# Starting the expert loops of a fused transformer kernel once their first groups of tokens are routed

## The reference, cut to what matters

```
# experts (stages 0 and 2)
logits = x @ router_w.T                         # [T, 8]
m1 = max(logits); gates1 = softmax(where((m1-logits)/max(|logits|,m1) > 0.02, -inf, logits))
mult1 = gates1[argmax]                          # the same once more without the winner: mult2
dense_w[tok, ind1] += mult1; dense_w[tok, ind2] += mult2
for e in range(8):
    h = silu(x @ w_gate[e].T) * (x @ w_up[e].T)             # 128 -> 256
    out += dense_w[:, e:e+1] * (h @ w_down[e].T)            # 256 -> 128
x = x + 0.5 * out                                # the kernel puts the 0.5 into the gates
# attention (stage 1), 16 heads of 8
attn = softmax(q k^T * 8**-0.5); out = (attn v) @ w_proj.T + b_proj
```

## Time and profile before

| | us |
|---|---|
| median of 3 executions | 2050.31 |
| the profiled execution | 2053.51 |
| its span, first to last instruction | 2051.7 |
| stage 0, front and routing | 0 to 65 |
| stage 0, expert loops | 65 to 361 |
| attention, preparation | 361 to 421 |
| attention, turns 0 to 15 | 421 to about 1097 |
| attention, turn 16 | about 1097 to 1145 |
| attention's end, front and routing of stage 2 | 1145 to 1207 |
| stage 2, expert loops | 1207 to 1507 |
| stages 3 to 5 | 1507 to 2052 |

### The profile page before, as it was taken

How to read it: one execution, slowest core, us unless ns; L and a number is a source line. 1 busy time by engine, 2 the same in 40 slices (tenths; PEclk the granted TensorE clock), 3 DMA queues, 4 the chain that set the end, 5 groups by cost and what they waited for, 6 DMA issues and landing times.

```text
span 2051.7 us, 31351 instructions
## 1 busy us (share of the span) xinstructions
PE 1710.9 (83%) x10673; PEld 980.1 (48%) x10673; DVE 1498.2 (73%) x2427; ACT 936.7 (46%) x1787; POOL 407.4 (20%) x716
## 2 busy tenths in 40 slices
PE   4799999549998999899898569999967669885675
PEld 3688888301111111111112358888845545553454
DVE  4655555689999999999992366555668848886884
ACT  2222222506887888788787322222234412111452
POOL 5311010310000100000000310100035642333442
PEclk9999999858999999999999769999987869997787
DMA  3000000210100011001100100000000000000000
GB/s 114 1 1 0 0 0 1 97 57 18 41 23 22 22 34 30 22 22 29 27 16 8 51 0 1 0 0 0 0 1 0 0 1 1 1 1 1 1 21 21
DMA packets 25450, 35.17 MB, mean 17 GB/s; under 512 B 6016, under 2 KB 20160, under 8 KB 24832
## 3 DMA queue, kind: packets, MB, share of 16 engines
q1 hardware_dynamic: 25344, 33.79, 5.6%
HBM read 20.80 MB, written 8.39 MB: 14 GB/s over the span
## 4 chain that ended last, share of the span: by engine, by line
PE 65%; DVE 17%; issue 5%; POOL 5%; ACT 5%; DMA 1%; POOLq 1%; DVEq 0%; SPq 0%; ACTq 0%
PE PS L744 12%; PE PS L312 11%; PE PS L732 9%; PE PS L301 6%; PE PS L302 6%; PE PS L303 6%; PE PS L721 5%; DVE neg_half L844 4%; DVE shared L1528 3%; PE PS L1281 3%; ACT probs L812 3%; DVE qk_all L1063 2%; PE PS L1393 1%; PE PS L1295 1%; DVE qk_all L1066 1%
## 5 line engine op out<-in xcount | busy, mean ns | idle before, releaser
L844 DVE TENSOR_REDUCE neg_half<-PS 128x2 f32<-128x1024 f32 x512 | 601.0, 1220 | 48.0 <-PE PS L721 33.1
L812 ACT ACTIVATE probs<-PS 128x512 f32<-128x512 f32 x1024 | 529.2, 604 | 184.8 <-PE PS L732 184.4
L363 ACT ACTIVATE shared<-PS 128x512 f32<-128x512 f32 x256 | 153.1, 598 | 425.9 <-PE PS L303 409.9
L477 DVE TENSOR_TENSOR shared<-shared,PS 128x512 f32<-128x512 f32 x256 | 175.8, 687 | 173.2 <-ACT shared L363 172.8
L732 PE MATMUL PS<-qk_all 51*128 51x512 bf16 x1024 | 279.7, 391 | 16.9 <-ACT probs L812 12.2
L744 PE MATMUL PS<-probs,Vg 128*32 128x512 f32 x2048 | 277.8, 615 | 0.1
L721 PE MATMUL PS<-qk_all 48*128 48x512 bf16 x1024 | 203.3, 408 | 60.4 <-DVE neg_half L844 39.4
L312 PEld LDWEIGHTS PS<-wd,shared 128*128 128x128 f32 x2048 | 247.9, 192 | 11.5
L312 PE MATMUL PS<-wd,shared 128*128 128x128 f32 x2048 | 248.6, 275 | 0.0
L732 PEld LDWEIGHTS PS<-qk_all 51*128 51x128 bf16 x1024 | 72.3, 94 | 343.5 <-ACT probs L812 326.1
L485 DVE SCALAR_TENSOR_TENSOR x<-PS,gates,x 128x128 f32 (+1 forms) x512 | 144.2, 344 | 72.7 <-PE PS L312 72.7
(11 more groups left out here) (194 smaller groups left out, 2321.8 us busy)
## 6 DMA issues: line engine op xcount, KB each, us to landing
split<-shared SPq DMA_DIRECT2D x16, 384.0 KB, 3.3
qk_all<-split SPq DMA_DIRECT2D x64, 96.0 KB
qk_all<-split SPq DMA_DIRECT2D x64, 64.0 KB
qk_all<-split SPq DMA_DIRECT2D x64, 32.0 KB
shared<-OTs SPq DMA_DIRECT2D x60, 32.0 KB
SC<-OTs SPq DMA_DIRECT2D x60, 32.0 KB
probs<-in_ret_const SPq DMA_DIRECT2D x1, 1538.5 KB, 6.8
qk_all<-negT SPq DMA_DIRECT2D x96, 4.0 KB, 1.8
```

The costliest lines, as they stand in the source:

```text
L363: act.activation(sg[:, f, :], bank(f), ACT.Silu).then_inc(s["silu"], 1)
L477: dve.tensor_tensor(h[:, FCH * (e % 2) + f, :], sg[:, f, :], bank(2 + f), ALU.mult).then_inc(s["h"], 1)
L812: act.activation(probs[:, n % 2, STRIPS * strip + pair, :], bank(RING_AT + use % RING), ACT.Exp, scale=ATT_SCALE).then_inc(s["exped"], 1)
L844: dve.tensor_reduce(neg_half[m % 2][:, i % 2, :, at], bank(use_bank(i, m), 2).rearrange("p (s w) -> p s w", s=STRIPS), AX.X, ALU.max, nega ...
```

## The change

- **The front.** Only the first 2 groups (stage 0) or 4 groups (stage 2), `HEAD`, are normalised, transposed, scored and routed ahead of the loops. The others pass through `first_group`, the loop over the 8 experts of group 0, at places given by `FRONTS`; one PSUM bank each for transposes (6) and logits (7). In stage 0 that is two groups in each of the experts 0, 1, 2; in stage 2 groups 4, 5, 6, 7 in experts 1, 2, 3, 5. The rest of the routing is a generator stepped on DVE in experts 4 to 7 (3, 3, 3, 4 steps) in stage 0 and 6, 7 (9, 4) in stage 2. Logits are taken from `xT`; the second copy `xTf` is gone.
- **Stage 2's head** lies in attention's turn 16, between its steps. The projection, addition and statistics of groups 6 and 7, and the last half's reciprocal, move into experts 0, 1 and 2 of `first_group`. POOL's `ln_finish` is written out between its attention work.
- **Routing.** The two rounds share one exponential over both; operations that do not depend on each other are not chained; two parts (head, rest).
- **Weights of stage 0.** hi and lo are made in 4 chunks of 512 columns, POOL's chunks alternating with `ln_finish` of two groups; x arrives in two transfers, the second behind the weights.
- **Reciprocals** of sequences 0 to 2. SP moves one row of denominators per head to DRAM, gathers 16x1024 into 128x128, DVE takes that reciprocal in turns 6, 10, 14 (step 1), SP writes it to DRAM and spreads it onto 128x1024; POOL multiplies in turns 7, 11, 15.
- FP4 weight steps go beside groups 6 and 7 of stage 2 in place of 0 and 7.

```diff
+        HEAD = {0: 2, 2: 4}
+        FRONTS = {0: {0: (2, 3), 1: (4, 5), 2: (6, 7)}, 2: {1: (4,), 2: (5,), 3: (6,), 5: (7,)}}
@@ moe_pe @@
+            def first_group():
+                left = None
+                for e in range(EXPERTS):
+                    if e + 1 < EXPERTS:
+                        if n == 0 and (e + 1) % 2 == 0:
+                            pe.wait_ge(ld["wlo"], e + 3)
+                        gate_up(0, e + 1, FCH * e + 1)
+                    else:
+                        pe.wait_ge(s["lo"], 2)
+                        gate_up(1, 0, FCH * e + 1)
+                    if left is not None:
+                        moe_logits(pe, n, left, 7)
+                        left = None
+                    fronts = FRONTS[n].get(e, ())
+                    if fronts:
+                        if n == 2:
+                            pe.wait_ge(att["added"], GROUPS - 1 if e < 3 else GROUPS)
+                        moe_transposes(pe, n, fronts[0], 6)
+                    down(0, e)
+                    if fronts:
+                        moe_logits(pe, n, fronts[0], 7)
+                    if len(fronts) > 1:
+                        moe_transposes(pe, n, fronts[1], 6)
+                        left = fronts[1]
+                    if n == 2 and e == 0:
+                        att_project(pe, GROUPS - 2, 6)
+                    if n == 2 and e == 2:
+                        pe.wait_ge(s["xT"], FRONTS[2][2][0] + 1)
+                        att_project(pe, GROUPS - 1, 6)
@@ moe_dve @@
+            def first_group():
+                rest = route(dve, chain, n, 1, s["gates"])
+                for e in range(EXPERTS):
+                    wait(dve, s["y"], e)
+                    hidden(e + 1, (e + 1) % EXPERTS)
+                    add(0, e)
+                    if n == 0 and e == 0:
+                        for g in range(4, GROUPS):
+                            ln_stats(dve, g)
+                    if n == 2 and e in (0, 2):
+                        g = GROUPS - 2 + e // 2
+                        att_add(dve, g, 6)
+                        dve.wait_ge(att["added"], g + 1)
+                        ln_stats(dve, g)
+                    if n == 2 and e == 1:
+                        att_reciprocals(dve, BATCH - 1, GW, SEQ)
+                    for g in FRONTS[n].get(e, ()):
+                        moe_scores(dve, n, g, 7)
+                    if e + 1 > n // 2:
+                        for g in FRONTS[n].get(e + 1, ()):
+                            moe_tokens(dve, n, g)
+                    for _ in range({0: (0, 0, 0, 0, 3, 3, 3, 4), 2: (0, 0, 0, 0, 0, 0, 9, 4)}[n][e]):
+                        next(rest)
...
+            head = route(dve, chain, n, 0, s["x_acc"])
+            for _ in range(9):
+                next(head)
             hidden(0, 0)
+            for _ in head:
+                pass
+            for g in FRONTS[n][n // 2]:
+                moe_tokens(dve, n, g)
+            first_group()
@@ moe_pool, stage 0 @@
+                for c in range(W_CHUNKS):
+                    weights_low(c)
+                    if c < W_CHUNKS - 1:
+                        ln_finish(pool, 0, 2 * c + 2)
+                        ln_finish(pool, 0, 2 * c + 3)
+                moe_low(pool, 0, 1)
@@ att_sp @@
+            def gather_sums(b):
+                sp.wait_ge(s["moved"], MOVED * HG * (b + 1))
+                wait(sp, s["spread"], 16 * b)
+                sp.dma_start(compact_sums[:, :], sums[b, :, :].rearrange("h (k w) -> (h k) w", k=HD)).then_inc(s["sums"], 16)
+            def spread_inverse(b):
+                sp.wait_ge(s["rec"], b + 1)
+                sp.dma_start(inverse[b, :, :].rearrange("h (k w) -> (h k) w", k=HD), compact_sums[:, :]).then_inc(s["inverse"], 16)
+                sp.wait_ge(s["inverse"], 16 * (b + 1))
+                wait(sp, s["on"], b)
+                sp.dma_start(SC[:, 0, :], inverse[b, :, :].unsqueeze(1).to_broadcast([HEADS, HD, SEQ])).then_inc(s["spread"], 16)
...
+                if i > HG and i % HG == 2:
+                    spread_inverse(i // HG - 1)
                 if 1 < i <= AG:
+                    r = i - 2
+                    if r < AG - HG:
+                        compact(r)
+                    else:
+                        compact_wide(r, 0, SEQ, s["moved"])
@@ att_pe, steps n of turn 16, g = n // 2 @@
+                        if n % 2 == 0 and 4 <= g < 4 + HEAD[2]:
+                            moe_logits(pe, 2, g - 4, LOGITS[2])
+                        if n % 2 == 0 and 3 <= g < 3 + HEAD[2]:
+                            moe_transposes(pe, 2, g - 3, TURNED[2])
@@ att_pool, after its loop @@
+            for g in range(HEAD[2]):
+                ln_finish(pool, 2, g)
+            moe_low(pool, 2, 0)
+            ln_finish(pool, 2, HEAD[2])
+            ln_finish(pool, 2, HEAD[2] + 1)
+            normalised(BATCH - 1, BATCH, 0, GW)
+            moe_low(pool, 2, 1)
+            ln_finish(pool, 2, GROUPS - 2)
+            normalised(BATCH - 1, BATCH + 1, GW, SEQ)
+            ln_finish(pool, 2, GROUPS - 1)
```

More of the change, by code:

```diff
@@ new lines, in moe_copy, with moe_logits @@
+        def moe_copy(act, n, g, b):
+            act.wait_ge(moe[n]["xT_ps"], g + 1)
+            act.activation(xT[:, g * GW:(g + 1) * GW], bank(b), ACT.Copy).then_inc(moe[n]["xT"], 1)
+        def moe_logits(pe, n, g, b):
+            s = moe[n]
+            pe.wait_ge(s["xT"], g + 1)
+            wait(pe, s["logits"], g)
+            for j in range(GT):
+                t = g * GT + j
+                last = pe.matmul(bank(b)[:, j * EXPERTS:(j + 1) * EXPERTS], xT[:, t * P:(t + 1) * P], wr[:, :],
+                                 start=True, stop=True)
+            last.then_inc(s["logit_ps"], 1)
@@ L271, in moe_pe @@
         def moe_pe(pe, n):
             s = moe[n]
-            def transposes(g, u):
-                pe.wait_ge(s["xn"], g + 1)
-                wait(pe, s["xT"], g - 1)
-                for j in range(GT):
-                    last = pe.transpose(bank(6 + u)[:, j * P:(j + 1) * P], xn[:, u, j * P:(j + 1) * P], ident[:, :])
-                last.then_inc(s["xT_ps"], 1)
-            def logits(g, u):
-                if more(g):
-                    transposes(g + 1, 1 - u)
-                pe.wait_ge(s["xTf"], g + 1)
-                wait(pe, s["logits"], g - 1)
-                for j in range(GT):
-                    last = pe.matmul(bank(4 + u)[:, j * EXPERTS:(j + 1) * EXPERTS], xTf[:, u, j * P:(j + 1) * P],
-                                     wr[:, :], start=True, stop=True)
-                last.then_inc(s["logit_ps"], 1)
@@ L290, in moe_pe @@
-            transposes(0, 0)
-            rolled(pe, logits)
             def gate_up(g, e, ready):
@@ L505, in moe_dve @@
+            for _ in head:
+                pass
+            dve.wait_ge(s["x_acc"], 1)
+            for g in FRONTS[n][n // 2]:
+                moe_tokens(dve, n, g)
+            first_group()
+            dve.wait_ge(s["gates"], 1)
+            before = GROUPS - 2 if n == 2 else GROUPS - 1
+            with dve.Fori(1, before) as g:
                 group(g, False)
-            group(GROUPS - 1, True)
+            for g in range(before, GROUPS):
+                group(g, g == GROUPS - 1)
             dve.wait_ge(s["x_acc"], E_LAST + 1)
@@ L746, in values @@
                 last.then_inc(s["pv"], 1)
-            def project(g):
-                pe.wait_ge(s["on"], max(g // 2, g - BATCH + 1) + 1)
-                pe.wait_ge(s["read"], len(NUMBER))
-                wait(pe, s["added"], g - JH + 1)
-                for j in range(GT):
-                    t = g * GT + j
-                    last = pe.matmul(bank(g % JH)[:, j * P:(j + 1) * P], OC[:, t * P:(t + 1) * P], wproj[:, :],
-                                     start=True, stop=True)
-                last.then_inc(s["proj"], 1)
             def turn(i, first, second, third):
@@ L1653, in _ @@
             ln_stats(dve, 0)
-            for name, first, last in (("x_half", 1, GROUPS // 2), ("x_rest", GROUPS // 2, GROUPS)):
-                dve.wait_ge(ld[name], 16)
-                with dve.Fori(first, last) as g:
-                    ln_stats(dve, g)
-            dve.wait_ge(ld["small"], 32)
+            ln_stats(dve, 1)
             moe_dve(dve, chain, 0)
```

355 lines of the change are left out of this document (221 added, 134 removed).

## The result

The changed kernel took 1977.49 us (median of four executions, 1976.24 to 1979.08), the kernel before 2050.56: a ratio of 0.9638, 95% interval 0.9626 to 0.9651. The forecast was 1976 (1959 to 2000). Run again beside later experiments, the changed kernel took 1981.2 (five executions, 1974.96 to 1987.97; ratio 0.9658, 0.9634 to 0.9681); of those 3.7 us more, 3.2 are in the kernel before too, which took 2053.7 beside it. What is its own is the spread: 13 us, against 3 us for the kernel before. That turned out to be the most interesting thing in this case.

What follows compares the result with a forecast made beforehand. Expert loops are PE-bound and unchanged; serial time in two routing fronts and three reciprocals goes: 20.9 + (22.8 - 3) + (38.5 - 2.5) = 76.7, less 2 unseen, off 2050.3 gives 1976 us, range 1959 to 2000.

Steps and rivals of the forecast that it cites:

- Reciprocals: 20.9 said: Attention, sequences 0 to 2: removing three wide reciprocals saves 23.9 us, three small ones cost 1.0 each; gain 20.9.
- 0.95 x 7.95 / 6.54: Attention: most that one added 128x128 reciprocal loses, scaled from the wide one's cost; 1.2 us, taken as 1.0.
- rival 2: Attention: compact reciprocals' transfers land late, 4 us at each of three sequences; 1988 us, or 1997 at worst; chance 0.07.
- Stage 0: 19.8 said: Stage 0: fourth add gains 25.2 us, 2.4 lost to the rest of routing, 3 to clock restarts.
- the fourth add of group 0 comes at 62.8: Stage 0: after POOL's chain come normalisation, h of expert 3, gate-up, logits, down; add at 62.8, today 87.99.
- Two engines, one port: Stage 0: POOL's operations hold DVE's routing operations for up to 1.26 us each; 0 to 3 us, taken as 1.5.
- the last part: List of signs in the trace; for stage 0, wrong if PE's idleness before the fourth add ends on anything but POOL's rstd.
- The clock's 3: Stage 0: one and a half TensorE clock restarts of about 2 us each, charged as 3 us.
- Turn 16 and stage 2: 36.0 said: Attention's end to group 1's second add: at 1219.9, today 1258.36; gain 38.5 us less 2.5 for clock restarts.
- Rival 1: First groups' expert loops crawl at half clock with queue waits: 36 us more, 2012; half of it, 1994, likelier; chance 0.16.
- Rival 3: Stage 0: late x transfer and POOL's serial chain keep the first group as late as today; 1996 us; chance 0.12.
- rival 4: Expert loops: TensorE stays at its low clock level after the first group, 56 experts x 4.1 us; 2206 us; chance 0.02.

Runs made afterwards that it cites:

- the two reciprocal kernels: Changed kernel with 128x1024 reciprocals put back for sequences 0 to 2, 2004.0 us; changed kernel with three more 128x128 reciprocals ahead of each compact one, 1993.2 us.
- logits apart: Changed kernel with the logits of turn 16's first three groups issued one step later, between the halves of the transposed scores; 1973.9 us, ratio 0.9634.
- fill: Changed kernel with three more 512-column matmuls ahead of the logits of each of the four groups in turn 16; 1986.0 us, ratio 0.9680.

## Why the prediction was right, and where it was not

The time was right, 1976 for 1977.5 (and 1981.2 later), and the mechanism was right: serial time in two fronts and three reciprocals, taken away while the loops stayed PE-bound. Its terms were less exact than its sum, and that the sum came out within 2 us was in part luck: stage 0 gave 5.5 us less than was said; the reciprocals and stage 2 gave 3.6 more, and the 2 us kept for things unseen were not needed.

- **Reciprocals: 20.9 said, 23.1 measured.** Removing them was worth what the half sets said, as the experiment that puts them back shows. The small one was charged 1.0 us each time and cost 0.17: DVE had that much slack. The sum was linear ("0.95 x 7.95 / 6.54"); measured were 0.17 for the first and 3.6 to 4.9 for the next three. (The row of 0.61 us that the prediction reads as one matmul covers two.) The transfers' room of 7.4 us was enough (rival 2 did not occur): the spread was issued at 671.19 and the evacuation at 680.03 was on time.
- **Stage 0: 19.8 said, 14.3 measured in the first profile, 16.5 to 17.0 in the repeated and the two reciprocal kernels (second add of group 1 at 98.7 to 99.1).** The step that failed is "the fourth add of group 0 comes at 62.8". The schedule followed POOL's queue to the rstd of group 7 and stopped there, "the end is 55". Behind it POOL goes on: a weight chunk, a lower half, two memsets of 5.26 us, and DVE's normalisation of exactly the groups that were just made ready lies beside them. The prediction had this effect in hand ("Two engines, one port") and charged 1.5 us for small operations in the routing; it didn't look for the large ones. Before, the memsets lay beside the loops and cost nothing. POOL's rstd was there at 51.5 and PE was idle until 60.71, for DVE's `xn` that the memset held; the last part had named any other end of that wait than rstd as a sign of being wrong.
- **It came out near because other terms were too dear.** Independent routing operations start 0.14 to 0.16 us apart (21.26, 21.40 and then 21.62, 21.76, 21.92, 22.05), only chained ones 0.26, so the head's routing ended at 25.8 and not at 27.5. POOL's chain from group 4 to 7 took 15.4 and not 16.5. The rest of the routing cost 0.95 and not 2.4 (28.58 us from the fourth add to the second of group 1, 27.63 before; by the prediction's own 0.40 us an operation the last expert's nine are 1.15 over and not 0.9). The clock's 3 were partly not needed: behind the first h TensorE worked at 1.2 GHz only for some 7 us of group 0, 47.0 to 50.4 and 60.7 to 64.0.
- **Turn 16 and stage 2: 36.0 said, 37.4 measured.** Turn 16 was charged 7 and took 9.0; with logits apart and the clock at 1.00 throughout it took 50.09, 5.4 more than before. From the last evacuation to the second add of group 1 1219.9 - 1151.5 = 68.4 was said and 67.4 measured. Of the nine routing steps 4.9 us were to show; 8.82 - 4.59 = 4.2 did, and the next interval (7.21) held the change of group as well. PE's gap at that change, said to be some 5 us, was 3.94.
- **The clock.** The prediction put its restarts where PE waits 2 to 5 us, in front of experts. The costly fall was elsewhere, in turn 16's second half, where no wait is longer than 0.53 us. In the first profile it cost about 2 us (1.93 for 1.06, 1.83 for 1.16 and the exponentials behind), in others some 8 more (36.3 against 28.4). Rival 1 named the right mechanism in the wrong place. By the rule on oscillation in the Trainium skill (TensorE: Matmul & The Clock Gate, "HAM oscillation — how this bites in real kernels") long waits between bursts are what keeps the clock low; no wait of that kind stands in turn 16, so the trace shows a fall that this rule does not cover.
- Rival 3 (stage 0 gains nothing) and rival 4 (the loops stay at the low level) did not occur: the loops' granted clock was 1.00 and experts came 4.59 us apart.

## What to carry to other kernels

When a schedule is moved, follow each engine's queue past the last thing that you need from it: what comes next in that queue now lies beside other work than before, and a cheap clearing operation can hold another engine for its whole length. A gain in a queue can be taken back by the next item of the same queue, so test such edits together as well as alone. Where medians spread over more than the effect looked for, read a milestone ahead of the noisy place in the trace, and then build the pair of kernels in which that place is quiet.

## What the runs showed of the hardware

- **GpSimd's memset blocks VectorE's TENSOR_SCALAR completely.** Two groups' normalisation beside two memsets took 14.22 (with three subtractions beside it as well), 11.66 and 10.03 us, without them 2.13 or 2.14; one operation behind one memset took 5.35 in place of 0.27. It goes by instruction: in the changed kernel the first memset must end near 55.36 + 5.26 = 60.6, and PE got the transposes of group 6 at 60.71; the second ends at 65.88, and DVE went on to h at 66.20. The memset has no input, so an operation of GpSimd that only writes is enough. Not every operation of VectorE is held: beside the same memsets statistics of x, and products (h) and adds with one input from PSUM, took their usual 0.86, 0.69 and 1.13 us. The Trainium skill (SBUF — State Buffer, "Who interferes with whom") says that VectorE in a two-port mode and GpSimd hold a shared pair of ports for a whole instruction, whoever comes first; by this rule the trace agrees, DVE's operations behind a running memset waiting for its end.
- **TensorE's clock fell between short waits.** With fp32 logits of 8 columns directly ahead of fp32 transposes of 128, and waits of at most 0.53 us, the granted clock went to 0.50 in turn 16's second half in all ten profiles that have them side by side, for 3 to 27 us in the seven without fill and up to 44 us with it; it fell in the pair itself or up to 2 us behind it. Moved apart, it stayed at 1.00 in one profile and fell only in the last microseconds in two. More matmuls of 512 columns ahead of the pair made it worse. The pair is not the only place: five profiles have a fall of 3.4 us at the start of the turn, without it. The cause is not settled.
- **A wait of 2 us on TensorE cost some 2.5 more**: after 2.01 and 0.52 us of idleness the granted clock was 0.50 from 663.4 to 670.2, the same eight records took 1.93 in place of 1.06, and the half set was 4.6 us longer for 2.05 us more of waiting.
